# A selective scan followed by a gated mixing layer, one core: the du stores moved ahead on the DMA queue, and eight decay units of the first chunk ahead of the first scan

## The reference

```python
x = x + attn(layernorm(x));  x = x + ffn(layernorm(x))
# attn, with u = layernorm(x):
deltaBC = u @ W_bc.T                       # 64 + 32 + 32 columns
delta = softplus(deltaBC[:, :64] @ W_dt.T + b_dt);  Bm, Cm = the other two
A = -exp(A_log)
h[t] = exp(delta[t] * A) * h[t-1] + (delta[t] * u[t]) * Bm[t]    # 256 x 32 states
y[t] = sum over states of h[t] * Cm[t]  + u[t] * D_param
```

## Time and profile before

| | |
|---|---|
| runs, median (lowest to highest) | 909.21 us (904.12 to 910.14) |
| the profiled execution | 912.55 us, span 910.8 us |
| DVE / PE / ACT / POOL busy | 89% / 85% / 54% / 51% of the span |
| DVE scans, L1817 | 585.5 us in 256 |
| first scan, last scan | at 66 us, at 720 us |
| mean granted TensorE clock | 0.959 |

### The profile page before, as it was taken

How to read it: one execution, slowest core, us unless ns; L and a number is a source line. 1 busy time by engine, 2 the same in 40 slices (tenths; PEclk the granted TensorE clock), 3 DMA queues, 4 the chain that set the end, 5 groups by cost and what they waited for, 6 DMA issues and landing times.

```text
span 910.8 us, 19855 instructions
## 1 busy us (share of the span) xinstructions
PE 775.3 (85%) x6396; PEld 546.6 (60%) x6396; DVE 809.7 (89%) x1027; ACT 491.8 (54%) x883; POOL 461.8 (51%) x782
## 2 busy tenths in 40 slices
PE   6668899888988898998899889988888678999985
PEld 5556566655655565655556565655555366887864
DVE  8707999998999899989999999999999948899884
ACT  4235746764675477557657655854444243455531
POOL 7504744755373457437554644663333724565354
PEclk9867999999999899999999999999999889999997
DMA  2942464264435444542653455365223352101002
GB/s 66 141 107 92 75 148 128 88 114 127 116 74 104 134 120 66 138 129 84 106 137 115 80 109 148 88 102 144 83 72 96 85 162 78 47 32 39 24 24 69
DMA packets 242693, 88.59 MB, mean 97 GB/s; under 512 B 164304, under 2 KB 235472, under 8 KB 242640
## 3 DMA queue, kind: packets, MB, share of 16 engines
q1 hardware_dynamic: 236304, 85.56, 39.0%
q10 hardware_dynamic: 6336, 2.36, 1.1%
HBM read 45.85 MB, written 42.04 MB: 96 GB/s over the span
## 4 chain that ended last, share of the span: by engine, by line
PE 31%; SPq 25%; DVE 17%; issue 12%; ACT 5%; DMA 4%; POOL 4%; ACTq 0%; DVEq 0%; POOLq 0%
PE psum L1445 10%; DVE arena L1817 9%; SPq L964 7%; PE psum L429 6%; PE psum L1355 5%; PE psum L1367 5%; SPq L972 5%; SPq L982 4%; SPq L985 4%; DMA du_terms<-umid_home 3%; POOL arena L370 3%; ACT arena L1579 2%; SPq L959 2%; PE psum L1288 2%; SPq L998 1%
## 5 line engine op out<-in xcount | busy, mean ns | idle before, releaser
L1817 DVE TENSOR_TENSOR_SCAN arena<-arena,psum 128x1024 f32<-128x1024 f32 x256 | 585.5, 2287 | 8.9
L1579 ACT ACTIVATE arena<-psum 128x512 f32<-128x512 f32 x512 | 279.2, 596 | 243.9 <-PE psum L1355 243.2
L1445 PE MATMUL psum<-du_mov,b_sta 96*128 96x128 bf16 x2048 | 272.4, 314 | 65.7 <-DVE arena L1817 64.1
L1445 PEld LDWEIGHTS psum<-du_mov,b_sta 96*128 96x128 bf16 x2048 | 206.6, 131 | 95.4 <-DVE arena L1817 93.8
L1233 POOL TENSOR_TENSOR carry<-arena 128x64 f32<-128x64 f32 x252 | 109.7, 435 | 289.0 <-ACT arena L1579 158.6
L1355 PEld LDWEIGHTS psum<-delta_mov,a_sta 96*128 96x128 bf16 x2048 | 133.1, 102 | 137.4 <-issue 96.0
L1355 PE MATMUL psum<-delta_mov,a_sta 96*128 96x128 bf16 x2048 | 168.0, 225 | 15.3 <-ACT arena L1579 8.4
L1367 PE MATMUL psum<-arena,c_sta 128*32 128x512 f32 x1024 | 148.7, 648 | 0.4 <-DVE arena L1817 0.4
L429 PE MATMUL psum<-delta_mov,arena 128*128 128x256 f32 (+6 forms) x544 | 115.1, 369 | 7.2 <-ACT arena L550 7.1
L429 PEld LDWEIGHTS psum<-delta_mov,arena 128*128 128x128 f32 x544 | 89.0, 195 | 29.2 <-ACT arena L550 9.1
L1814 DVE TENSOR_TENSOR psum<-psum,carry 128x64 f32<-128x64 f32 x256 | 54.0, 211 | 41.9 <-PE psum L1445 37.0
(11 more groups left out here) (172 smaller groups left out, 794.8 us busy)
## 6 DMA issues: line engine op xcount, KB each, us to landing
du_mov<-du_terms SPq DMA_DIRECT2D x128, 96.0 KB
delta_mov<-delta_terms SPq DMA_DIRECT2D x128, 64.0 KB
y<-y_rows SPq DMA_DIRECT2D x32, 256.0 KB
du_terms<-arena SPq DMA_DIRECT2D x28, 256.0 KB, 5.3
delta_terms<-arena SPq DMA_DIRECT2D x48, 128.0 KB, 6.4
b_sta<-b_terms SPq DMA_DIRECT2D x128, 48.0 KB
b_terms<-small SPq DMA_DIRECT2D x42, 128.0 KB, 2.3
arena<-in_L_attn_x SPq DMA_DIRECT2D x8, 512.0 KB, 4.2
```

The source lines that it names most:

```text
L1445: mm = nc.tensor.matmul(sub(psum, 0, P, o, (1, 4), (TS, GD // 2)), b_sta[k][0:ROWS, (s * 4 + tg) * P:(s * 4 + tg + 1) * P], sub(du_mov[k], ...
L1579: nc.scalar.activation(sub(arena, 0, P, u * 16 * TS, (TS, 16), (decay_at(k, 1), SUBS), (1, TS)), sub(psum, 0, P, (4 + u % 2) * BANK, (TC, ...
L1817: nc.vector.tensor_tensor_scan(arena[:, STATE_AT[s] + o:STATE_AT[s] + o + GD * TS], arena[:, decay_at(k, s) + o:decay_at(k, s) + o + GD * TS],
```

## The change

Three edits. (1) Of chunk 0's 16 decay units, 8 instead of 12 are made ahead of the first step, and the other 8 behind the products of step 1 instead of behind those of step 0; the spare matmuls between them are gone. (2) The stores of uhi move from chunk 2 to the end of chunk 1, behind the last delta store. (3) The stores of umid move to the head of chunk 2, ahead of `store_b`; the store of ulo alone stays behind `store_y`, now with the wait for `b_stored` in front of it.

```diff
-        FIRST_UNITS = 3 * UNITS // GROUPS
+        FIRST_UNITS = UNITS // 2
...
             if first and kk == 0 and step < AHEAD:
-                return [(0, u) for u in range(FIRST_UNITS, UNITS)] if step == 0 else []
+                return [(0, u) for u in range(FIRST_UNITS, UNITS)] if step == 1 else []
...
                     if late and kk == 2:
+                        settle(sp_)
+                        sp_.wait_ge(S["umid_ready"], p)
+                        store_du(p, 1, "u_stored")
                         settle(sp_)
                         sp_.wait_ge(S["args_ready"], (c + 1) * UNITS)
                         store_b(p, NEW, "b_stored")
...
                         sp_.wait_ge(S["dlo_ready"], p)
                         store_delta(p, NEW, 2, "d_stored")
+                        settle(sp_)
+                        sp_.wait_ge(S["uhi_ready"], p)
+                        store_du(p, 0, "uhi_stored")
                     if late and kk == 2:
-                        for part, ready, done in ((0, "uhi_ready", "uhi_stored"), (2, "ulo_ready", "u_stored"),
-                                                  (1, "umid_ready", "u_stored")):
-                            settle(sp_)
-                            sp_.wait_ge(S[ready], p)
-                            store_du(p, part, done)
-                            if part == 0:
-                                settle(sp_)
-                                sp_.wait_ge(S["b_stored"], 16 * TERMS * p)
+                        settle(sp_)
+                        sp_.wait_ge(S["b_stored"], 16 * TERMS * p)
+                        settle(sp_)
+                        sp_.wait_ge(S["ulo_ready"], p)
+                        store_du(p, 2, "u_stored")
...
                                 mm = decay_args(c + ahead, (k + ahead) % 2, u, True)
-                                if start and not ahead:
-                                    spare(1, 6)
```

## The result

| | before | changed |
|---|---|---|
| median of 8 runs each, side by side (lowest to highest) | 907.91 us (904.12 to 912.92) | 916.22 us (908.42 to 918.78) |
| ratio | 1 | 1.0068, interval 1.0037 to 1.0099 |
| the profiled execution | 912.55 us | 911.84 us |
| DVE's carry adds, first to last | 66.0 to 720.1 us | 63.0 to 718.6 us |

The changed kernel is slower by 0.7%, where I had forecast 900.5 us and a gain. (A ratio here is computed from the single executions, those of the chip's slower state left out, and not from the medians; the quotient of these two is 1.0092.) Its profiled execution lies 4.4 us under its own median, and that of before 3.3 to 4.6 us above its own. So the two traces are nearly equal in time, and serve to see what waits for what; the medians say how much.

A forecast was written before the change was run, and what follows sets the result against it. DVE was taken to set the pace from the first scan to the last, losing time to `take_z`'s wait for umid's stores. Forecast: 912.55 - 11.8 (tiles) + 1.6 (overruns) - 1.8 (start) = 900.55 us; own range 895 to 905, wider range 895 to 920.

The forecast's parts named there:

- the price of the wait: DVE's waits for products inside the scans, nine places: all 11.8 us taken as gained once `take_z` starts earlier.
- I let it land in 3.9 us: Last du store, tile 2: lands 3.9 us after its issue begins, the profiled row's value.
- 298.4 + s: Tile 2's last du store: landing at 298.4 plus s, the shift of `load_md`; 303.0 in all.
- the rival of 0.13: Last du store lands as late as now, `take_z` near 306, tiles gain nothing, start 1.8: 907.4 us; chance 0.13.
- the shift of `load_md`: Five stores now ahead of `load_md` delay it by s = 4.6 us, between bounds of 3.0 and 6.9.
- the rule: If the five stores' 1.31 MB must pass before `load_md`'s first row, at 207 GB/s, s is 6.3 us.
- The cover of tile 2: Chunk 3, step 2: `load_md` lands at 297.6, PE takes it up at 301.22; 3.6 us spare.
- PE's lead of 1.25 us: Step 3's products end 1.25 us before DVE takes them, so s is free up to about 4.85.
- This pattern stands in seven tiles: Tile 2's cover and lead for `load_md` were taken to hold in tiles 0 to 6.
- 0.23 us a tile: Charge for small overruns of `load_md`'s cover: 0.23 us in each of seven tiles, 1.6 us.
- the two rivals: `load_md` becomes the late one, 927 us (chance 0.22); the last store lands as late as now, 907.4 (0.13).
- the start: Chunk 0, fewer units ahead of the first products: first add at 63.4 instead of 66.04, gain 1.8 us.

The follow-up runs named there:

- `v_both_early`: Against the kernel before, no start edit: uhi's stores at the end of chunk 1, umid's and ulo's ahead of `load_md`, `store_b` behind it; 901.21 us, ratio 0.9901.
- `ulo_ahead_of_y`: Store edits alone, with ulo's store directly behind `load_md` and ahead of `store_y`, start as before; 906.05 us, ratio 0.9914 to the kernel before.
- `e2_stores`: Kernel before with the store edits alone (second and third), start as before; 915.73 us, ratio 1.006.
- `six_ahead`: Kernel before with all six du stores ahead of `store_b` and `load_md`, start as before; 914.8 us, ratio 1.0041.
- `start_spares`: `v_both_early` plus the start edit, with a spare matmul kept behind each of the eight units; 898.48 us, ratio 0.9823 to the kernel before.
- `e3_changed`: The changed kernel run and profiled once more, beside the kernel before; 915.64 us, ratio 1.0054.
- `both_early_2`: `v_both_early` run again on another chip, beside the kernel before; 900.22 us, ratio 0.9849.

## Why the prediction was wrong, point by point

**Right: the bound and the price of the wait.** DVE's idle time inside the tiles is worth about what it measures, and `take_z`'s wait is its cause: `v_both_early` takes both away and gets 12.8 us in the stretch of the scans (11.8 forecast).

**Wrong, and this decides it: "I let it land in 3.9 us", "298.4 + s" = 303.0.** Tile 2's last du store was issued at 298.38, 0.7 us before the 294.45 + 4.6 of the forecast, so its place on the queue was right. It landed 6.9 us after its issue and not 3.9, and tile 2 is the mildest case: in the seven tiles it is 6.9 to 9.3 us. Counted from the load's first issue, the forecast has the store land after 298.4 - 287.07 = 11.3 us; measured are 14.2 to 15.9. The row I took the 3.9 from, umid at 302.55, was a store that came 9 us after `store_y` at 293.56, when the load was done by my own estimate (297.6). The moved one comes 1.8 us after the load's last issue (296.55), while PE can't start on the load until 301.83, and a `store_y` of 256 KB stands between. `ulo_ahead_of_y` shows what the forecast had wrong: with `store_y` behind instead of ahead the same store lands after 11.8 us, nearly as forecast, `take_z`'s wait is gone and the ratio is 0.9914 instead of the 1.006 of `e2_stores`.

A row with the same predecessor stands in the trace of before, but it is ambiguous. The first uhi store there, issued at 294.45 behind `load_md` and `store_y`, is given a landing 4.1 us later, and the third, issued at 295.60, one 8.6 us later. The three add to one semaphore, and `take_z` needs all three, so the landing that counts is the last, at 304.2. That is 6.6 us behind my 297.6 for the load, for `store_y` and three du stores, 1.65 us each. Two of them behind a load that lands at 297.6 + 4.6 give 305.5 (an estimate), where 305.3 was measured.

I had this outcome as the rival of 0.13 ("ulo's part in the two engines that `load_md` keeps busy waits for it"). I set it low on the grounds that 0.5 MB instead of 1.8 is behind the load. The table shows what that left out: the 1.3 MB taken away there save 3.6 us, and they stand in front of the load instead, for 4.3 us. The prediction had both numbers in it as separate terms (s = 4.6, and 298.4 without a shift) and never set the one against what it bought.

**Half right: the shift of `load_md`.** s was forecast at 4.6, with 6.3 for the rule that the stores' data must pass first; the load's first issue moved by 4.3 us on average. The time from chunk 1's `store_y` to chunk 2's shows it tile by tile. Before, in tile 1:

```profile
188.01 1.13 SPq L1024 DMA_DIRECT2D y<-y_rows  x1
...
209.15 0.64 SPq L1024 DMA_DIRECT2D y<-y_rows  x1
```

and of the changed kernel:

```profile
186.79 1.30 SPq L1024 DMA_DIRECT2D y<-y_rows  x1
...
213.11 0.64 SPq L1024 DMA_DIRECT2D y<-y_rows  x1
```

21.1 us became 26.3, s = 5.2; in tile 2 (272.53 to 293.56, 272.52 to 297.42) s = 3.9, and in the others 3.7 to 4.3. So the issue times were the better measure in six tiles, and tile 1 lies between them and the rule's 6.3. The cover of tile 2 was as worked out: the load begun 4.0 us later is there at 301.83, with PE idle for 0.18 us. PE's lead of 1.25 us held too: in tile 1 it idled 2.22 us and DVE 0.96, a difference of 1.26. What failed is **"This pattern stands in seven tiles"** and "0.23 us a tile": I measured cover and shift in one tile and took them for all. PE waited in all seven, up to 2.22 us, and in `e2_stores` tile 1 had 2.92. The load itself took 10.2 to 11.6 us from its first issue until PE could start, by tile, where I had 10.5. "Tile 2, the worst of the six" holds for DVE's waits alone; `take_z` waited longest in tile 1 (4.71 us).

**Not in the prediction: the two rivals together.** I priced them as alternatives. They meet at chunk 3, steps 2 and 5, of the same tile, and ACT's exps, PE's units and the clock are common to both: a PE that has lost its lead at step 2 has less to lose at step 3. `ulo_ahead_of_y` has the late load alone (0.9914), the kernel before the late store alone, the change both (1.0054 to 1.0068). That the sum is more than before's one wait is measured; how it divides between lost lead and the clock's falls (0.50 at 226 to 228 us) stays open. `six_ahead`, whose one late transfer is `load_md` as in `ulo_ahead_of_y`, gives 1.0041 and not 0.9914. Its load begins later by one more store, about 1 us in five of seven tiles (in tile 2 19.5 us behind chunk 1's `store_y` against 18.5). PE's waits in the tiles are 15.7 us against 8.8, over its lead of 1.25 us in seven tiles against two, and DVE's are 13.1 us against 4.9. So DVE loses more than in proportion once the load is past the lead; no run varies the load's start alone.

**Right as far as can be told: the start.** 1.8 forecast, 2.1 and 2.2 between medians, neither clear of noise by itself; first add at 62.98 (63.4 forecast), step 2's at 71.80 (72.6 to 73.0), with 0.46 us of both from PE's earlier first unit. What I had not named is the releaser, POOL's carry (L1236), and step 3's 0.75 us. That the clock may stay low longer without the spare matmuls came true, as `start_spares` shows, and did not take the gain back.

**The sum.** 912.55 - 11.8 + 1.6 - 1.8 = 900.55 forecast against 911.84 profiled, 11.3 apart. Instead of 11.8 gained and 1.6 charged, 10.2, the tiles lost 0.65 (12.45 against 11.8): 10.85 of the 11.3. The rivals' 927 and 907.4 start from the median of 909.21 and not from the 912.55 of this sum; from 912.55 the late store gives 910.75, 1.1 from the profiled time. The medians add 4 us that this execution did not have. `e3_changed`, with 915.0 us of span, shows 2.3 of it in the stretch of the adds (657.9 us against 655.6): 13.45 us of waits for products in the tiles (37.3 - 23.1 - 0.75) and 1.0 for POOL. The rest is open. `v_both_early`, without any such wait, lies 9.7 us under the median of before and not 12.8, so a usual execution of before may wait some 3 us less in its tiles than the profiled one (an estimate); no run's profile shows one.

**What would show it.** Of the signs of being wrong, "PE waiting for DMA `delta_mov<-delta_terms` inside the scans" and the clock of 0.50 at chunk 3 (in tile 1, at 226 to 228 us) came; of those of being right, the last du store near 299 and the first add near 63.4. DVE's waits at 23 to 25 us in one or two places and `take_z` released by POOL did not come. The median of 916.2 lay inside 895 to 920, but with 0.48 for no difference and 0.35 for faster the direction that is measured had the least weight.

## What to carry to other kernels

The landing time of a DMA is a property of what stands ahead of it on the queue. Take it from rows with the same predecessors, counted from where the predecessor lands, and where several stores share a semaphore, from the last of them. When transfers are moved ahead of a load, set what they save behind it against what they cost in front of it: here 3.6 us against 4.3. List the deadline of everything on the queue and put what nobody wants soon (here `store_b` and `store_y`) behind both critical transfers. With both there the kernel gained 1.0 to 1.5%, and with `store_y` alone 0.9%, where swapping one lateness for another lost 0.7%. Work out cover and shift in each tile, and price two rivals that meet at the same place as one case of their own.

## What was not expected of the hardware

In tile 2 one DMA store of 256 KB landed 6.9 us after its issue behind `load_md` (41 GB/s, share 0.12) and a `store_y` of the same size, 3.5 us after PE could start on the load. Put directly behind the load it landed 5.4 us after its issue, 0.7 us after PE could start (301.07). Over seven tiles it is 3.2 to 5.0 us against 0.6 to 0.8.

The same code waits more in one launch than in another: of the changed kernel, the profiled execution of 911.84 us has 12.45 us of DVE's waits in the tiles, and that of 916.82 has 13.45 and 1.0 more for POOL. So one profile of such a kernel can lie 4 us beside its median, as here. The kernel before had 904.25 to 918.47 us in 28 runs on one chip, and `v_both_early` 899.2 to 901.51 in six on the same; on another chip it was 907.01 to 920.03 in 14 against 897.43 to 903.38 in six (`both_early_2`). That the waits are what spreads the runs of the kernel before fits this and is not shown.
